# FFN of an attention block: the up projection through ScalarE and GpSimd in place of VectorE

## The reference

```
scale = max(max|block| / 6, 1e-12)
xq    = nearest of {0, .5, 1, 1.5, 2, 3, 4, 6} to |x / scale|, times sign and scale

gate = xq @ wq_gate.T          # 256 -> 704
up   = xq @ wq_up.T            # 256 -> 704
h    = silu(gate) * up         # 704 wide
out  = x + quantised(h) @ wq_down.T
```

## Time and profile before

| | us |
|---|---|
| median of 3 runs | 454.61 (454.4 to 455.08) |
| the profiled execution | 453.78 |
| its span | 451.6 |

### The profile page before, as it was taken

How to read it: one execution, slowest core, us unless ns; L and a number is a source line. 1 busy time by engine, 2 the same in 40 slices (tenths; PEclk the granted TensorE clock), 3 DMA queues, 4 the chain that set the end, 5 groups by cost and what they waited for, 6 DMA issues and landing times.

```text
span 451.6 us, 9319 instructions
## 1 busy us (share of the span) xinstructions
PE 387.9 (86%) x3581; PEld 306.9 (68%) x3581; DVE 346.3 (77%) x677; ACT 277.4 (61%) x859; POOL 206.9 (46%) x183
## 2 busy tenths in 40 slices
PE   1889759999999999999999999996487797788955
PEld 1568638877878878778788788884256565566744
DVE  2789886777876687678766879778868998998792
ACT  3497757678777876787778767855224435424421
POOL 8250033263353442633535423513557778777841
PEclk9999988999999999999999999999888999999998
DMA  7960000000000000000000000000000000000011
GB/s 240 320 220 1 2 0 1 1 1 1 3 1 2 1 1 3 1 1 2 1 1 1 2 1 2 0 2 0 1 1 1 23 14 12 25 13 12 25 36 35
DMA packets 8426, 11.46 MB, mean 25 GB/s; under 512 B 499, under 2 KB 6335, under 8 KB 8383
## 3 DMA queue, kind: packets, MB, share of 16 engines
q1 hardware_dynamic: 8383, 10.88, 7.5%
HBM read 8.78 MB, written 2.10 MB: 24 GB/s over the span
## 4 chain that ended last, share of the span: by engine, by line
DVE 38%; PE 34%; POOL 10%; ACT 10%; issue 6%; DMA 1%; SPq 0%; POOLq 0%; ACTq 0%; DVEq 0%
PE ps L351 9%; PE ps L353 8%; PE ps L352 8%; POOL arena L1163 4%; PE ps L451 4%; PE ps L443 4%; DVE arena L934 4%; DVE negmax L925 3%; ACT arena L672 3%; DVE arena L984 3%; DVE arena L916 3%; DVE arena L986 3%; DVE vw L870 3%; DVE blk_h L951 2%; DVE arena L1072 2%
## 5 line engine op out<-in xcount | busy, mean ns | idle before, releaser
L1155 POOL TENSOR_TENSOR arena<-arena,rinv 128x616 f32<-128x616 f32 x64 | 77.6, 1213 | 148.6 <-DVE rinv L930 148.6
L351 PE MATMUL ps<-vw,arena 128*128 128x256 f16 (+1 forms) x352 | 98.0, 278 | 12.3 <-DVE arena L823 6.1
L672 ACT ACTIVATE arena<-ps,negmax 128x154 f32<-128x154 f32 x256 | 96.0, 397 | 18.0 <-DVE negmax L925 17.7
L352 PE MATMUL ps<-vw,arena 128*128 128x256 f16 (+1 forms) x352 | 97.8, 278 | 0.0
L353 PE MATMUL ps<-vw,arena 128*128 128x256 f16 (+1 forms) x352 | 97.7, 277 | 0.0
L934 DVE TENSOR_TENSOR arena<-ps,arena 128x512 f16<-128x512 f32 x80 | 54.9, 686 | 18.7 <-ACT arena L682 18.5
L682 ACT ACTIVATE arena<-ps 128x512 f16<-128x512 f32 x80 | 48.5, 606 | 25.2 <-PE ps L451 24.0
L351 PE MATMUL ps<-arena,xnT_h 128*128 128x352 f16 x128 | 41.2, 322 | 18.1 <-DVE xnT_l L994 16.3
L925 DVE TENSOR_REDUCE negmax<-ps 128x4 f32<-128x616 f32 x64 | 50.6, 792 | 6.8 <-PE ps L443 5.6
L672 ACT ACTIVATION_READ_ACCUMULATOR arena<-ps,negmax 128x1 f32 x256 | 55.1, 215 | 0.0
L451 PE MATMUL ps<-ident,arena 128*128 128x128 f32 x320 | 52.1, 286 | 0.0
(11 more groups left out here) (135 smaller groups left out, 903.7 us busy)
## 6 DMA issues: line engine op xcount, KB each, us to landing
out_dram<-arena SPq DMA_DIRECT2D x16, 128.0 KB, 1.7
xs<-in_x_dram SPq DMA_DIRECT2D x2, 896.0 KB, 10.0
arena<-in_L_xattn_w_out_dram SPq DMA_DIRECT2D x1, 1024.0 KB, 6.3
wffn<-in_L_ffn_w_down_dram SPq DMA_DIRECT2D x1, 704.0 KB, 7.9
wffn<-in_L_ffn_w_gate_dram SPq DMA_DIRECT2D x1, 640.0 KB, 11.0
wffn<-in_L_ffn_w_up_dram SPq DMA_DIRECT2D x1, 640.0 KB, 5.5
vw<-in_ctx_dram SPq DMA_DIRECT2D x1, 308.0 KB
xs<-in_x_dram SPq DMA_DIRECT2D x2, 128.0 KB, 4.9
```

The lines of the kernel that those rows point to most:

```text
L351: pe.matmul(o, a_h, b_h, start=start, stop=False)
L352: pe.matmul(o, a_h, b_l, start=False, stop=False)
L672: last = act.activation(prob[:, s, h * L:(h + 1) * L], ps[:, 2 * (j % 2) + k % 2, (k // 2) * L:(k // 2 + 1) * L], ACT.Exp, bias=negmax[:, ...
L1155: pool.tensor_tensor(v, v, rinv[:, s, 4 * j:4 * j + 4].unsqueeze(2).to_broadcast([P, 4, L]), ALU.mult).then_inc(normed, 1)
```

## The change

ACT's `silu_gate` gets a second instruction, which copies the up projection out of banks 2 and 3 into `hid`, scaled by 1/32. A new function on POOL, `gated`, multiplies `hid` with `silu` in place. DVE's `hidden` is removed. `up_done`, given by the copy, takes the place of `silu_done`, and is what PE's next `gate_up` waits for. `hid_ready` now comes from POOL. Since `silu` and `hid` are read on POOL, `silu_gate` waits for the product of the tile before and for `value_h` of the tile two before. The order also changes: on DVE `grid_h` of the tile before goes ahead of `scales_h`, on POOL `round_h` of the tile before goes ahead of `value_h`.

```diff
@@ PE, gate_up
-                wait(pe, hid_ready, t)
+                wait(pe, up_done, t)
@@ PE, turn_h, for the tiles that use other banks
-                    pe.wait_ge(hid_ready, 2 * STEPS)
+                    pe.wait_ge(up_done, 2 * STEPS)
@@ ACT
             def silu_gate(i, s):
                 act.wait_ge(gu_mm, 2 * i + s + 1)
-                act.activation(silu.rearrange("p (m n) -> p m n", m=2), ps[:, 0:2, 0:GU], ACT.Silu,
-                               scale=1.0 / FS).then_inc(silu_done, 1)
+                wait(act, hid_ready, 2 * i + s)
+                wait(act, hvalued, 2 * i + s - 1)
+                act.activation(silu.rearrange("p (m n) -> p m n", m=2), ps[:, 0:2, 0:GU], ACT.Silu, scale=1.0 / FS)
+                act.activation(hid[:, s].rearrange("p (m n) -> p m n", m=2), ps[:, 2:4, 0:GU], ACT.Copy,
+                               scale=1.0 / FS).then_inc(up_done, 1)
@@ DVE
-            def hidden(i, s):
-                t = 2 * i + s
-                dve.wait_ge(silu_done, t + 1)
-                dve.scalar_tensor_tensor(hid[:, s].rearrange("p (m n) -> p m n", m=2), ps[:, 2:4, 0:GU], 1.0 / FS,
-                                         silu.rearrange("p (m n) -> p m n", m=2), ALU.mult, ALU.mult).then_inc(hid_ready, 1)
@@ DVE, ffn
                     if s == 0 and exists(i + 1): grid_x(i + 1)
-                    hidden(i, s)
                     if not (peeled(i, 0) and s == 0) and exists(shift(i, s, 1)[0]): xq_low(*shift(i, s, 1))
+                    if exists(shift(i, s, -1)[0]): grid_h(*shift(i, s, -1))
                     scales_h(i, s)
...
-                    if exists(shift(i, s, -1)[0]): grid_h(*shift(i, s, -1))
@@ POOL
+            def gated(i, s):
+                pool.wait_ge(up_done, 2 * i + s + 1)
+                pool.tensor_tensor(hid[:, s], hid[:, s], silu, ALU.mult).then_inc(hid_ready, 1)
@@ POOL, ffn
                     if s == 0 and exists(i + 1): round_x(i + 1)
+                    gated(i, s)
+                    if exists(shift(i, s, -1)[0]): round_h(*shift(i, s, -1))
                     if not last_tile(i, s): value_h(i, s)
                     if s == 1 and exists(i + 2): value_x(i + 2)
-                    if exists(shift(i, s, -1)[0]): round_h(*shift(i, s, -1))
```

More of the change, by code:

```diff
@@ L221, in xattn_ffn_kernel @@
         xqt_mm, xqt_high, xqt_low = sem("xqt_mm"), sem("xqt_high"), sem("xqt_low")
-        gu_mm, silu_done, hid_ready = sem("gu_mm"), sem("silu_done"), sem("hid_ready")
+        gu_mm, up_done, hid_ready = sem("gu_mm"), sem("up_done"), sem("hid_ready")
         hscaled, hlowered, hvalued = sem("hscaled"), sem("hlowered"), sem("hvalued")
```

## The result

The changed kernel takes 476.94 us (median of 4, 476.82 to 477.5), the one before 454.5 in the same comparison: 1.0497 times as long, 95% interval 1.0479 to 1.0515. The forecast was 475 (461 to 484). The profiled execution has 476.87 and a span of 475.1.

What follows compares the result with a forecast made beforehand. DVE was taken as the bound, partly waiting for POOL; the moved work forms a ring between them. Start +3.1, four pairs +12.6 and tail +4.9, together +20.6 on 453.78, gave 474.4, stated as 475 us (461 to 484).

Steps and rivals of the forecast that it cites:

- The ring of the prediction: FFN steady part: POOL and DVE hand work to and fro, so a pair of tiles takes 19.5 us instead of 16.36.
- the exclusion: DVE instructions with two SBUF operands and POOL instructions reading SBUF run in turn; about 4 us blocked a pair.
- the rival of dependencies and length alone: Stated with the follow-up runs: only dependencies and POOL's added length cost time, so freeing the port leaves 477 us.
- The rival of a lock at half cost: FFN pairs: instructions meet less often, about 17.5 us a pair, total +11, 465 us; chance 0.10.
- first tiles: FFN start, through value_x of tiles 1 to 3: +3.1 us.
- the four pairs: FFN steady part, four pairs of tiles at +3.15 us each: +12.6 us.
- the last pairs: FFN tail, from the last value_x to the last tile's own quantisation: +4.9 us over 27.99.
- the rest: Everything behind the start of the last tile's own quantisation: nothing changes, 0 us.
- Product on POOL: Each 704-wide product of two SBUF operands on POOL takes 1.55 us, bounds 1.38 and 2.01.
- ScalarE's copy: ACT's 704-wide copy out of PSUM after each silu: 0.75 us, bounds 0.65 and 0.80; only its delay counts.
- PE's clock: Rival: gaps lower PE's clock, up to 6 us more a pair, two such pairs giving 486 us; chance 0.10.
- Signs: Expected in the changed profile, such as POOL over 80% busy in the steady part and L953 on 44 elements about 1 us.

Runs made afterwards that it cites:

- a_reduce: Changed kernel with the two grid_h instructions on DVE replaced by one-operand block maxima of the same 704 elements; 459.38 us, 1.0101 of the kernel before.
- a_memset: Changed kernel with POOL's product replaced by a memset of 1904 elements elsewhere, about as long but reading nothing from SBUF; 459.43 us, 1.0099 of the kernel before.
- a_old_order: Changed kernel with grid_h and round_h back in the places they have in the kernel before; 483.9 us, 1.0639 of the kernel before.
- b_new_order: Kernel before with only the change's order of grid_h and round_h, the product staying on DVE; 456.94 us, 1.0069 of the kernel before.

## Why the prediction was right

The mechanism. The ring of the prediction had, in the even tile: grid_h's first instruction ahead of the product, the product blocked, the second one blocked by it; in the odd tile the product first and grid_h behind it. The profile has this order in every pair of the steady part. The two experiments that keep lengths and waits and take away the exclusion, from DVE's side (a_reduce) and from POOL's side (a_memset), give 459.4 both, and the rival of dependencies and length alone, which wanted 477 of both, has fallen for the change's order. With the old order (a_old_order) it is that rival that describes the product. The rival of a lock at half cost has fallen too: a pair takes 19.9, not 17.5.

The number. That 475 came within 1.9 us of 476.94 is in part luck. The sum had +20.6 and the spans differ by 23.5. The first tiles were short by 1.6, the four pairs by 1.7, the last pairs by 0.6, and 1.7 of scatter in the attention part came on top; the rest, taken as 0, gave back 2.6.

The steps and their sizes:

- Product on POOL: I took 1.55 through two rows; it is 1.68. One of the rows had a float16 result. The estimate scaled from the Trainium skill's figure (GPSIMD Engine Reference, "Elementwise — side-by-side cycle accounting"; 1.55) was as low. Two products a pair make 0.26 of the 0.4 us by which the ring was too short. Of the rest, 0.06 is L987 behind the product in the odd tile (0.75 where I had 0.69), and some hundredths came in at hand-overs.
- First tiles: +4.65, and I had +3.1. Of the missing 1.6 us one instruction, which I had not put into the ledger, makes 1.5. DVE's timeline and POOL's, in the second tile of the changed kernel:

```profile
315.77 1.67 POOL L1196 TENSOR_TENSOR arena<-arena 128x704 f32<-128x704 f32 x1
...
315.83 1.64 DVE L851 TENSOR_TENSOR ln<-stats 128x4 f32<-128x4 f32 x1
```

A DVE instruction on 4 elements of the layernorm, with two operands in SBUF, waits for the product: 1.64 us, 0.15 in the kernel before (there L848), 1.63 in a_reduce. DVE was on the path there: it works without a pause from 312.44 to 326.79, the end of the scales that value_x needs. a_memset is no test of this, for there L851 takes 0.15 but L852 waits in its place (1.44).
- The rest: -2.6, and I had "nothing changes". In the kernel before, the last tile's six instructions on DVE took 6.74 us (434.49 to 441.23), with POOL's round_h and add_x1 beside them; in the changed kernel they took 5.19 (460.58 to 465.77), with one add beside them in place of three. That is 1.6 of the 2.6. The other 1.0 lies behind them, where PE's clock in the kernel before was lower: the granted clock from there to the end was 0.83, and 0.93 in the changed kernel. The last transposes, in the kernel before and in the changed one:

```profile
441.29 1.54 PE L563 MATMUL ps<-ident,arena 128*128 128x128 f32 x6 [3.16 <-DVE arena L1102]
...
466.12 0.82 PE L563 MATMUL ps<-ident,arena 128*128 128x128 f32 x6
```

Both parts come with the order, not with the product: in b_new_order the six take 5.24 and what follows 9.31 (9.33 in the changed kernel, 10.37 before).
- ScalarE's copy: 0.75, as taken, and covered. PE and the early up_done: covered, since the product never waited.
- PE's clock: 0.91 in the steady part, 0.97 before. It did fall, but POOL never stood idle before the product, so PE's clock cost nothing in the ring. The figure is close to the 0.9 below which I had called the forecast wrong.
- The order was charged as part of the ring. Alone it costs 2.9 us (b_new_order), and the product moved with the old order costs 29.5 (a_old_order).
- Signs: POOL was to be busy over 80% of the steady part, and was 68% (54.21 of 79.68). The sign didn't follow from the ring, whose POOL instructions with their waits add up to about 13.5 of 19.5 us. The scale on 44 elements was to take about 1 us and takes 0.74, ending with round_h as expected. The other signs came.

The rule of the Trainium skill (SBUF — State Buffer, "Who interferes with whom") is borne out in a point that the trace before did not show: a GpSimd instruction that only writes does not exclude a two-operand one of VectorE (0.89 in a_memset).

That a tiny instruction waits as long as a large one was in the trace before already (L953, 1.26 us on 32 elements); 1.64 us for 4 elements shows it again.

## What to carry to other kernels

Before work is moved from VectorE to GpSimd, list what VectorE runs at the same time with two SBUF operands, or as a small scale in SBUF: beside a GpSimd instruction that reads SBUF these don't overlap, and a PSUM operand in the old form may be what kept it free. The shares of idle and busy time of the two engines say nothing on this; stretched durations of single instructions, ending just after the other engine's, say it. Then look at what VectorE has to do until GpSimd's result is there: with nothing in between it stands idle for the whole of GpSimd's queue (47.4 us in a_old_order). Where two engines hand work to and fro, write down the ring with what blocks what before summing busy time, small instructions too.

## What was not expected of the hardware

- A memset of 1904 float32 on GpSimd takes 1.69 us and runs beside VectorE's two-operand instructions without stretching either (0.89). A VectorE TENSOR_SCALAR of 128x4 waited for such a memset all the same (1.44 us, 0.17 else).
- A VectorE TENSOR_TENSOR of 128x4 waited 1.49 us for GpSimd's 704-wide product.
- The GpSimd product of two full float32 operands costs 1.68 us for 704 elements (2.39 ns each), the one with a broadcast scale 1.39 (1.97 ns each).
